# Moving the first transposes and matmuls of a feed-forward stage into the tail of a Mamba-style stage, one Trainium2 core

## What is computed

```python
# sublayer 1: Mamba-2 mixer, 64 heads in 8 groups; last step of each group:
out = jnp.einsum('bli,di->bld', yn, out_proj_w)        # yn: gated and normalised heads
x = x + _layernorm(out)
# sublayer 2: feed-forward, 512 -> 1792 -> 512, weights are -1, 0, 1 with a scale per row
h = _layernorm(x)
gate_out = h @ (gate_t * gate_s[:, None]).T
up_out = h @ (up_t * up_s[:, None]).T
hidden = jax.nn.silu(gate_out) * up_out
x = x + _layernorm(hidden @ (down_t * down_s[:, None]).T)
```

## Time and profile before

| | |
|---|---|
| median of 3 runs | 1736.45 us (1735.08 to 1738.42) |
| the profiled execution | 1735.23 us |
| its span, first to last instruction | 1733.5 us |
| TensorE busy, mean granted clock | 1551.4 us (89%), 0.954 |
| DVE, ACT, POOL busy | 1225.2, 827.2, 947.4 us |
| last output product ends, first feed-forward matmul starts | 1010.7, 1028.58 us |
| feed-forward matmuls end (7 pairs) | about 1188 us |

### The profile page before, as it was taken

One profiled execution on the slowest core, in us unless ns is written; L12 is line 12 of the kernel. 1 busy time (PEld: TensorE's weight loads), 2 busy tenths in 40 slices (PEclk: granted clock), 3 DMA queues, 4 the chain that ended last, 5 costly groups with the idle time before them and its releaser, 6 DMA issues.

```text
span 1733.5 us, 26612 instructions
## 1 busy us (share of the span) xinstructions
PE 1551.4 (89%) x8870; PEld 1216.9 (70%) x8870; DVE 1225.2 (71%) x2024; ACT 827.2 (48%) x1639; POOL 947.4 (55%) x861
## 2 busy tenths in 40 slices
PE   3789999999999999999999869994889999987791
PEld 2567877877878778778787658883667676766681
DVE  5568878788788787877887866557467677768425
ACT  2355554554555545545545423331166667663231
POOL 3257667576676675766766851005443334427544
PEclk9899999999999999999999979997899999997796
DMA  3102111011021110120211022231000000042344
GB/s 117 37 5 87 33 49 58 17 48 64 13 86 31 48 57 16 48 67 12 89 27 48 20 80 73 73 97 36 0 14 1 14 1 2 1 171 74 122 138 165
DMA packets 49498, 92.60 MB, mean 53 GB/s; under 512 B 8017, under 2 KB 32721, under 8 KB 44177
## 3 DMA queue, kind: packets, MB, share of 16 engines
q1 hardware_dynamic: 45744, 79.58, 14.4%
q0 software_dynamic: 3680, 12.06, 2.1%
HBM read 81.14 MB, written 10.49 MB: 53 GB/s over the span
## 4 chain that ended last, share of the span: by engine, by line
PE 60%; DVE 15%; POOL 8%; issue 7%; ACT 5%; DMA 3%; SPq 1%; POOLq 0%; ACTq 0%; DVEq 0%
PE banks L355 29%; PE banks L1728 6%; DVE tap L1202 3%; PE banks L1854 3%; PE banks L1738 3%; PE banks L1819 2%; PE banks L1620 2%; PE banks L1652 2%; PE banks L1646 2%; DMA x<-in_w_gate 2%; PE banks L1844 2%; POOL wol L360 2%; PE banks L1661 2%; DVE acc L623 1%; DVE nmax L1440 1%
## 5 line engine op out<-in xcount | busy, mean ns | idle before, releaser
L1202 DVE SCALAR_TENSOR_TENSOR tap<-banks,parg,tap 128x511 f32<-128x511 f32 (+2 forms) x288 | 215.2, 747 | 39.0 <-ACT tap L927 31.8
L710 POOL TENSOR_TENSOR am<-ah,upto 128x1024 fp32r<-128x1024 f32 x64 | 121.9, 1905 | 187.4 <-PE banks L1620 138.2
L862 POOL TENSOR_SCALAR kz<-kst,head 128x512 fp32r<-128x512 f32 x64 | 99.1, 1567 | 159.9 <-DVE kst L1429 159.9
L355 PE MATMUL banks<-xTh,wch 128*128 128x512 f32 x384 | 162.4, 423 | 4.6 <-DVE em L1302 4.6
L935 ACT ACTIVATE th<-tap 128x512 f32<-128x512 f32 x96 | 60.7, 632 | 212.3 <-DVE tap L1202 210.2
L355 PE MATMUL banks<-xTh,wcl 128*128 128x512 f32 x384 | 150.9, 393 | 0.0
L355 PE MATMUL banks<-xTl,wch 128*128 128x512 f32 x384 | 150.0, 391 | 0.0
L1134 ACT ACTIVATE prob<-banks,nmax 128x128 f32<-128x128 f32 (+3 forms) x256 | 121.8, 530 | 54.6 <-DVE nmax L1440 54.4
L1440 DVE TENSOR_REDUCE nmax<-banks 128x2 f32<-128x256 f32 (+3 forms) x128 | 104.8, 819 | 40.3 <-PE banks L1845 40.2
L710 POOL TENSOR_TENSOR am<-al,upto 128x1024 fp32r<-128x1024 f32 x64 | 122.3, 1911 | 0.0
L1302 DVE TENSOR_TENSOR em<-banks,gmask 128x1024 f32<-128x1024 f32 x64 | 78.2, 1222 | 50.7 <-ACT banks L970 49.8
(11 more groups left out here) (289 smaller groups left out, 4476.8 us busy)
## 6 DMA issues: line engine op xcount, KB each, us to landing
x<-grownT SPq DMA_DIRECT2D x96, 128.0 KB, 4.7
x<-in_w_conv SPq DMA_DIRECT2D x7, 1536.0 KB, 6.6
x<-in_w_gate SPq DMA_DIRECT2D x8, 1024.0 KB, 4.9
x<-in_w_out SPq DMA_DIRECT2D x8, 1024.0 KB, 4.7
eraw<-in_expert_w SPq DMA_DIRECT2D x8, 1024.0 KB, 6.9
gur<-in_ff_gu SPq DMA_DIRECT2D x7, 1024.0 KB, 4.8
x<-in_hidden SPq DMA_DIRECT2D x16, 256.0 KB, 3.9
mates<-yd SPq DMA_DIRECT2D x8, 512.0 KB, 4.5
```

The costliest lines, as they stand in the source:

```text
L355: m = nc.tensor.matmul(o, a, b, start=first and n == 0, stop=last and n == len(terms) - 1)
L710: m = pool.tensor_tensor(am[:, part, :, :], a[:, i, :].bitcast(F32).unsqueeze(2).to_broadcast([P, HG, P]), upto[:, :].unsqueeze(1).to_broa ...
L862: m = pool.tensor_scalar(kz[:, quad % 2, p2, j, :], kst[:, p2, :].bitcast(F32), head[:, j:j + 1], None, ALU.mult)
L1202: nc.vector.scalar_tensor_tensor(tap[:, q % 2, sh:L], bk(CONV_BANKS[q % 2])[:, 0:L - sh], parg[:, KC * q + k:KC * q + k + 1], tap[:, q % 2 ...
```

## The change

1. TensorE issues `norm_turn(1, 0)` to `(1, 2)` at the start of step 8 and `(1, 3)` at the start of step 9. ACT's `norm_high` of tiles 0 to 2 is at the start of step 8 (behind `weights_high(0)`), of tile 3 in step 9. DVE's `norm_low` of tiles 0 to 2 is at the end of step 8, of tile 3 at the start of step 9. The transposes use other banks (`turned`), so the first five wait for no low part.
2. In step 9 TensorE issues the first quarter (`half(0, 0, True)`, 16 matmuls) in front of the output product of tile 7; it waits for the low part of tile 3 and for the cast weights. Behind the output product come turns 4 and 5, the second quarter, turns 6 and 7, and then quarters three and four, which wait for all low parts.
3. ACT casts the first pair's weights at the end of step 7. SP loads them between the `grown` loads of tiles 5 and 6, and loads the scales right behind the last tiles of x.
4. DVE makes `fsc` behind round 7 and no longer behind round 10; `norm_low(4)` stands in front of round 8, and one low part follows each later round. The wait for `consts` 8 and POOL's list are as before.
5. `up_ps` isn't incremented ahead of time any more, and the waits on it count one less.

```diff
+        def turned(q, i):
+            return bk((5, 2, 3, 0, 4, 5, 4, 5)[i] if q == 1 else i % 2)
...
-            for i in (3, 5, 6, 7):
+            for i in (3, 5):
+                grown_load(G - 1, i)
+            if STAGES >= 2:
+                sp.wait_ge(h_ready, NB * CT * G)
+                sp.dma_start(gur[:, :, :, :, :], ff_gu[0]).then_inc(gu_in, 16)
+                sp.dma_start(dnr[:, :, :], ff_dn[0]).then_inc(dn_in, 16)
+            for i in (6, 7):
                 grown_load(G - 1, i)
...
             if STAGES >= 2:
-                sp.wait_ge(h_ready, NB * CT * G)
-                sp.dma_start(gur[:, :, :, :, :], ff_gu[0]).then_inc(gu_in, 16)
-                sp.dma_start(dnr[:, :, :], ff_dn[0]).then_inc(dn_in, 16)
-                tile_done(sp, 1, NT - 1)
...
-            lag, made = 4 if q else 2, 0
+            lag, made = 4 if q else 2, CH if q == 1 else 0
+            if q == 1:
+                norm_low(q, CH)
+                made += 1
...
-                while q < STAGES and made <= n - lag and made < (NT if n == NT + lag - 1 else 2 * (n - start) + 2):
+                while q < STAGES and made <= n - lag:
                     norm_low(q, made)
                     made += 1
...
-                norm_wait(nc.tensor, q, "lo", i - 1)
+            freed = (0, 0, 0, 0, 0, 1, 5, 6)[i] if q == 1 else i - 1
+            if freed > 0:
+                norm_wait(nc.tensor, q, "lo", freed)
             for k in range(KT):
-                mmi = nc.tensor.transpose(bk(i % 2)[:, k * P:(k + 1) * P], acc[:, i, k * P:(k + 1) * P], ident[:, :])
+                mmi = nc.tensor.transpose(turned(q, i)[:, k * P:(k + 1) * P], acc[:, i, k * P:(k + 1) * P], ident[:, :])
             mmi.then_inc(nsem["tr"], 1)
...
+                if last and s == NT:
+                    for j in range(CH - 1):
+                        norm_high(1, j)
+                if last and s == NT + 1:
+                    norm_high(1, CH - 1)
...
+                if s == NT - 1 and last and STAGES >= 2:
+                    weights_high(0)
...
-            norm_scalar(1) if STAGES >= 2 else None
+            for i in range(CH, NT):
+                norm_high(1, i)
...
+                if last and s == NT + 1:
+                    norm_low(1, CH - 1)
...
+                if last and s == NT:
+                    for j in range(CH - 1):
+                        norm_low(1, j)
             group_steps(dve, step)
-            norm_vector(1, NT)
             if STAGES >= 2:
                 dve.wait_ge(small_in, 16 * 11)
                 chain(nc.vector.tensor_scalar(fsc[:, 0, :], gus[:, 0, :], 0.5, None, ALU.mult))
                 nc.vector.tensor_tensor(fsc[:, 1, :], fsc[:, 0, :], gus[:, 1, :], ALU.mult).then_inc(f_part, 1)
+            norm_vector(1, NT)
+            if STAGES >= 2:
                 dve.wait_ge(f_part, 1)
...
+                if last and s == NT:
+                    pe.wait_ge(m_ready, NT * G)
+                    for i in range(CH - 1):
+                        norm_turn(1, i)
+                if last and s == NT + 1:
+                    norm_turn(1, CH - 1)
...
+                if last and s == NT + 1 and STAGES >= 2:
+                    norm_wait(pe, 1, "lo", CH)
+                    pe.wait_ge(gu_cast, KT)
+                    half(0, 0, True)
...
-                tile_done(pe, 1, NT - 1)
-                norm_tensor(1)
-                norm_wait(pe, 1, "lo", NT)
...
-                def hidden_pair(f, first):
+                def hidden_pair(f):
                     pe.wait_ge(gu_cast, KT * f + KT)
-                    gate_up(f, 0, first)
-                    if not first:
-                        down(f - 1, 1)
-                    gate_up(f, 1, first)
+                    half(f, 0, False)
+                    half(f, 1, False)
+                    down(f - 1, 1)
+                    half(f, 2, False)
+                    half(f, 3, False)
                     pe.wait_ge(dn_cast, 2 * f + 2)
                     down(f, 0)
-                hidden_pair(0, True)
+                pe.wait_ge(ssv_ready, NT * G)
+                for i in range(CH, CH + 2):
+                    norm_turn(1, i)
+                tile_done(pe, 1, NT - 1)
+                half(0, 1, True)
+                for i in range(CH + 2, NT):
+                    norm_turn(1, i)
+                norm_wait(pe, 1, "lo", NT)
+                half(0, 2, True)
+                half(0, 3, True)
+                pe.wait_ge(dn_cast, 2)
+                down(0, 0)
                 with pe.Fori(1, FP) as f:
-                    hidden_pair(f, False)
+                    hidden_pair(f)
```

More of the change, by code:

```diff
@@ L682, in norm_tensor, with norm_high @@
                 norm_turn(q, i)
+        def norm_high(q, i):
+            norm_wait(nc.scalar, q, "tr", i + 1)
+            nc.scalar.copy(xTh[:, :, i * P:(i + 1) * P],
+                           turned(q, i).rearrange("p (k t) -> p k t", k=KT)).then_inc(nsem["hi"], 1)
         def norm_scalar(q):
             for i in range(NT):
[L686 to L688 removed]
+                norm_high(q, i)
         @block.gpsimd
@@ L941, in gate_tanh, with weights_high @@
                 nc.scalar.activation(gt, bk(bank), ACT.Tanh, scale=0.5).then_inc(tg_ready, 1)
+            def weights_high(f):
+                act.wait_ge(gu_in, 16 * f + 16)
+                for k in range(KT):
+                    nc.scalar.copy(gu[:, k, :, :, :], gur[:, k, :, :, :]).then_inc(gu_cast, 1)
             def step(g, s, first, last):
@@ L1054, in _, with hidden_pair @@
             group_steps(act, step)
-            norm_scalar(1) if STAGES >= 2 else None
+            for i in range(CH, NT):
+                norm_high(1, i)
             if STAGES >= 2:
-                def hidden_pair(f):
-                    act.wait_ge(up_ps, 4 * f + 1)
-                    act.wait_ge(gu_in, 16 * f + 16)
-                    for k in range(KT):
-                        nc.scalar.copy(gu[:, k, :, :, :], gur[:, k, :, :, :]).then_inc(gu_cast, 1)
+                def hidden_pair(f, first):
+                    if not first:
+                        act.wait_ge(up_ps, 4 * f)
+                        weights_high(f)
                     act.wait_ge(fsc_ready, f + 1)
@@ L1075, in hidden_pair @@
                                 nc.scalar.copy(hid_part(hidh, r), hidf[:, r % 2, :]).then_inc(hid_hi, 1)
-                with act.Fori(0, FP) as f:
-                    hidden_pair(f)
+                hidden_pair(0, True)
+                with act.Fori(1, FP) as f:
+                    hidden_pair(f, False)
             if STAGES >= 3:
@@ L1592, in gated, with half @@
                                     for k in range(KT)]).then_inc(gate_ready, 1)
+            def half(f, q, first):
+                b, ft = q // 2, q % 2
+                tok = slice(b * L, (b + 1) * L)
+                if not (first and q < 2):
+                    pe.wait_ge(hid_f, 4 * f + q - 1)
+                for w, done in ((0, gate_ps), (1, up_ps)):
+                    for k in range(KT):
+                        for part in (xTh, xTl):
+                            m = mat(bk(2 * w + ft), gu[:, k, ft, w, :], part[:, k, tok],
+                                    start=(k == 0 and part is xTh), stop=(k == KT - 1 and part is xTl))
+                    m.then_inc(done, 1)
             def step(g, s, first, last):
@@ L1713, in _ @@
             if STAGES >= 2:
-                tile_done(pe, 1, NT - 1)
-                norm_tensor(1)
-                norm_wait(pe, 1, "lo", NT)
-                def gate_up(f, b, first):
-                    tok = slice(b * L, (b + 1) * L)
-                    for ft in range(2):
-                        q = 2 * b + ft
-                        if not (first and q < 2):
-                            pe.wait_ge(hid_f, 4 * f + q - 1)
-                        for w, done in ((0, gate_ps), (1, up_ps)):
-                            for k in range(KT):
-                                for part in (xTh, xTl):
-                                    m = mat(bk(2 * w + ft), gu[:, k, ft, w, :], part[:, k, tok],
-                                            start=(k == 0 and part is xTh), stop=(k == KT - 1 and part is xTl))
-                            m.then_inc(done, 1)
                 def down(f, b):
```

9 lines of the change are left out of this document (2 added, 7 removed).

## The result

The changed kernel takes 1746.83 us, median of 5 runs (1744.67 to 1748.33); the kernel before, in 5 runs, 1737.78 (1735.08 to 1740.29). The ratio is 1.0053, 95% interval [1.0041, 1.0065]: 7.1 to 11.3 us slower. The three runs of the table further up are among these five; the two later ones move the kernel's median from 1736.45 to 1737.78. The profiled execution of the changed kernel took 1744.67 us.

What follows compares the result with a forecast made beforehand. Bound: TensorE's standstill at the stage border and its clock afterwards. Third quarter +4.4 to +7.9 later, plus its half-speed +1.6 to +2.75, gives +6.0 to +10.7; middle +8.4 on 1736.45 is 1744.8, range 1740.0 to 1748.5.

Steps and rivals of the forecast that it cites:

- Step 8: Three transposes in front: TensorE waits 3.5 us for tile 2's input, restarts at half speed; tile 6's addition +3.6 to +4.8.
- Step 9: First quarter in front of the last output product delays tile 7's addition behind tile 6's by 8.8 to 9.95 us more.
- Behind T: From T, the start of DVE's addition of tile 7: third quarter at T + 19.85 to 21.0, before T + 27.85.
- The clearing: POOL's 3.51 us clearing of `acc` waits for turn 7 and holds `fscg`, delaying the third quarter; price 2.2 to 3.
- the clearing is no bound: Rival at the end of DVE's chain: chain late anyway or clearing overlapped; 2.2 comes off, +6.2, 1742.7; chance 0.08.
- Third quarter: After a pause of 5 us it runs first at half speed, before at full: +1.6 to +2.75.
- The sum: All terms together: +6.0 with short half-speed stretches, +10.7 with long ones; middle +8.4 taken.
- The clock stays up: Rival at TensorE's four starts: 2.4 GHz kept throughout; -0.4, 1736.1, not slower; chance 0.09.
- A further stall at `fsc`: Rival: `fsc`, now in front of three rounds, is held 2.1 more; +8.1 to +12.8, 1744.6 to 1749.2; chance 0.10.
- Edits at nothing: Early weight loads hidden by room in SP's list; `fsc` behind round 7 takes 0.2 us in a 1.9 us gap.

Runs made afterwards that it cites:

- turns_behind: Changed kernel with only step 8's three transposes behind the output product of tile 6 and ACT's three high parts behind its high part of tile 7; 1741.87 us, ratio 1.0034.
- q1_behind: Changed kernel with only the first quarter put back behind the output product of tile 7; 1739.77 us, ratio 1.0013 to the kernel before.
- both_behind: Changed kernel with step 8's three transposes behind tile 6's output product and the first quarter behind tile 7's; 1735.35 us, ratio 0.9998 to the kernel before.
- clear_by_tile: Changed kernel with POOL's clearing of acc cut into 8 pieces, each behind its own tile's transpose; 1743.94 us, ratio 1.0035 to the kernel before.
- the filler: Changed kernel plus 20 matmuls that nothing reads, in TensorE's pause ahead of the third quarter; 1742.39 us, ratio 1.0032 to the kernel before.
- the placed versions: All of the change, but every transpose and the quarter behind the output products, clearing whole or in 8 pieces; ratios 0.9959 to 0.9971 to the kernel before.
- placed_again: The same kernel as placed_only, measured once more; 1731.43 us, ratio 0.9971 to the kernel before.
- placed_only: All of the change, but with every transpose and the quarter behind the output products, clearing in one piece; 1728.49 us, ratio 0.9962 to the kernel before.
- placed_and_cleared: The placing of placed_only, with the clearing of acc cut into 8 pieces of one tile; 1728.74 us, ratio 0.9962 to the kernel before.
- cleared_again: The same kernel as placed_and_cleared, measured once more; 1727.81 us, ratio 0.9959 to the kernel before.

## Why the prediction was right, point by point

Forecast 1744.8 us, measured 1746.83, inside the range of 1740.0 to 1748.5; +8.4 against +9.1 by the profile and +9.2 by the ratio. Of the 2.0 us between the two times 1.3 is the kernel before, whose median rose from 1736.45 to 1737.78, and 0.7 is the sum.

- *Step 8, +3.6 to +4.8:* measured +4.6 (12.81 less 8.20). The pause was 3.47 us (3.5 said), ACT's four casts and high parts were hidden as said (they ended at 1002.8, 1 us later than said, since the third high part waits for the third transpose), and turns_behind takes the whole term away. The cause is shown.
- *Step 9, +8.8 to +9.95:* +8.9 (14.34 less 5.46). Its pieces: 5.81 from the addition to the quarter (5.95 said), 5.59 for the 16 matmuls (5.25 to 6.4), 2.94 to the addition (3.05). q1_behind shows that the quarter's place is most of it, and that the fourth transpose alone holds 2.8 (8.27 less 5.46; 3.8 in both_behind), a share the prediction had not split off. It also let the half-speed stretch begin at the quarter. It began at the fourth transpose, 2.8 us earlier, so that only 3.9 us of it fell on the quarter: this term came in near its low end. That the quarter would be held by the low part of tile 3 came true (1.46 us).
- *Behind T, third quarter at T + 19.85 to 21.0:* T + 20.94. The details were less good than the total. I had one start at half speed, at turn 5. The trace has two pauses, 3.16 us in front of turn 4 and 2.90 in front of turn 5, and the clock is 0.50 from 1028.33 to 1037.64. So every matmul through two thirds of the second quarter was slow, which is why T + 20.94 is at the long end.
- *The clearing, 2.2 to 3:* 2.1, by clear_by_tile, just under the range. The rival "the clearing is no bound" is out: DVE's `fscg` was released by it, with ACT's tanh behind that.
- *Third quarter, +1.6 to +2.75:* +2.55 (9.87 from its start to the first down matmul, 7.32 before), and the filler gives back 2.4 of it.
- *The sum:* 4.6 + 8.9 - 6.9 + 2.55 = 9.15, where 6.9 is 27.85 less 20.94. The middles of the predicted terms are 4.2, 9.4, -7.4 and 2.2. So three terms came 0.4 to 0.5 above their middle and step 9 came 0.5 below, which leaves the missing 0.7. The half-speed stretches lasted 5.8, 6.7, 9.3 and 5.1 us after their starts, against a predicted 3.4 to 5.9. That the total came so near is in part luck: stretches of the same start vary by 2 us between two executions of one kernel (below), and the prediction had no way to know which it would get.
- *The clock stays up:* out, all four starts were at 0.50. The Trainium skill (TensorE: Matmul & The Clock Gate, HAM oscillation — how this bites in real kernels) has short bursts between waits start at the low clock each time, and this trace agrees. It isn't so each time in the other traces: the third quarter of clear_by_tile began at 1.00 behind a pause of 3.96.
- *A further stall at `fsc`:* out in this kernel, 0.17 and 0.18 us. It was a near miss, as the placed versions show (below).
- *Edits at nothing:* the early loads and casts cost nothing, as said; that they are worth 2.4 us by themselves was not in the prediction. The first quarter's casts left the path, and the sum had this inside its term for the third quarter's start (T + 27.85 before) without naming it.

## What to carry to other kernels

Filling an engine's idle time with work from the next stage paid here only behind the instruction on which the chain of waits hangs: put in front of it, the work charges its own length and its own wait for its input, and the pauses it makes are paid a second time in clock. Before moving such work, ask what it waits for at that point; here the change with the transposes and the quarter in front of the output products cost 9 us, and with them behind it gained 5 to 7, of which 2.4 is due to the early loads and casts. Afterwards look for what had been hidden in the old gap (here a clearing of 3.51 us), since it comes out into the open.

## What the runs showed of the hardware that was not expected

**Small DVE instructions held by POOL.** The second `fsc` instruction reads two 128x14 tiles. In the changed kernel it took 0.18 us, and POOL's addition to x began 0.3 us behind its end. In placed_again it began 0.11 us behind the addition's start:

```profile
1017.32 1.28 POOL L674 TENSOR_TENSOR x<-x,acc 128x512 f32<-128x512 f32 x1
...
1017.43 1.20 DVE L1393 TENSOR_TENSOR fsc<-fsc,gus 128x14 f32<-128x14 f32 x1
```

It ends with the addition (1018.63 and 1018.60), and it took 1.19 in placed_only and in both versions with pieces. The Trainium skill (SBUF — State Buffer, Who interferes with whom) says that a DVE instruction with two SBUF inputs contends with a GpSimd one that reads SBUF; this row agrees. The input of tile 7 beside the clearings took 3.02 us in clear_by_tile, 2.11 in placed_and_cleared, and 2.86 in cleared_again:

```profile
1020.98 2.84 POOL L805 MEMSET acc<- 128x512 f32 x6
1021.24 2.86 DVE L633 TENSOR_SCALAR acc<-x,mv,rs 128x512 f32<-128x512 f32 x1
...
1024.14 0.53 POOL L805 MEMSET acc<- 128x512 f32 x1 [0.32 <-PE banks L686]
```

It has one SBUF input besides the two scalars of each row, and POOL only writes. The same page lists `tensor_scalar` among the operations that can take both ports and then block for a whole instruction. The row agrees that it is held, but it is held until all six clearings are over, not just the one that was running. In cleared_again the transpose of tile 7 then waited 0.3 us for it, so clearing in pieces gives part of its gain back. The long clearing in one piece did the same to `fsc` before: what 2.34 us looked like there was a wait.

**The clock differs between two executions of the same kernel, at the same instruction and behind the same pause.** The output product of tile 7, behind a pause of 1.08 us, began at 1.00 in placed_only and at 0.50 in placed_again (rows above); it fell to 0.50 behind its third matmul in the kernel before. placed_and_cleared and cleared_again, again one kernel, kept 0.50 for 2.9 and for 5.2 us at the third quarter, behind pauses of 3.96 and 3.79. Step 7, ahead of everything that was moved on TensorE, took 12.09 us from DVE's addition of tile 4 to that of tile 5 in placed_only and 9.70 in placed_again. The fourth transpose and what follows it stayed low for 3.4 us in q1_behind, 5.6 in both_behind, 6.7 in the changed kernel and 8.9 in turns_behind (the last two with a second pause of 1.46 in between), and the start of tile 4's transpose for 9.3, with a second pause of 2.90. A start behind a pause of 3.96 (the third quarter of clear_by_tile) even began at full speed and fell to half 0.6 us later. After the filler the clock stood at 1.00 through a pause of 1.59. So the length of such a stretch can't be read from a kernel's order, nor from one trace of it; an estimate should carry both ends, and a difference of 1 to 2 us between two traces isn't yet one between two kernels.
